# First FFN's context rounded and subtracted one place earlier, attention steps divided anew, bias added later

## The reference

```python
x = x + 0.5 * ffn(layernorm(x))
x = x + attn(layernorm(x))        # 16 heads of 8, qkv and output bias
x = x + 0.5 * ffn(layernorm(x))

def ffn(x):                       # a switch head: H = 8 heads, E = 8 experts, P = 128
    gate_v, gate_o = top2_gates(x @ sel_v_w.T), top2_gates(x @ sel_o_w.T)
    q, k = x @ q_w.T, x @ k_w.T                       # by head
    v = sum_e (x @ v_w[h, e]) * gate_v[..., h, e]
    ctx = softmax(q @ k.T / sqrt(128)) @ v
    return sum_he (ctx[h] * gate_o[..., h, e]) @ o_w[h, e]
```

## Time and profile before

| | |
|---|---|
| three runs | 1562.11, 1564.19, 1565.19 us; median 1564.19 |
| the profiled execution | 1565.24 us; span of its instructions 1563.5 us |
| busy | PE 94%, DVE 84%, ACT 77%, POOL 62% of the span |
| mean granted clock of PE | 0.976 of full speed |
| first FFN's slots, up to the first attention score | to 660 us |
| last slots of the first FFN with 30 attention steps | 660 to 711 us |
| attention alone | 711 to 905 us |

### The profile page before, as it was taken

One profiled execution on the slowest core, in us unless ns is written; L12 is line 12 of the kernel. 1 busy time (PEld: TensorE's weight loads), 2 busy tenths in 40 slices (PEclk: granted clock), 3 DMA queues, 4 the chain that ended last, 5 costly groups with the idle time before them and its releaser, 6 DMA issues. The chain is left out here.

```text
span 1563.5 us, 25918 instructions
## 1 busy us (share of the span) xinstructions
PE 1474.1 (94%) x7227; PEld 1101.0 (70%) x7227; DVE 1308.9 (84%) x3532; ACT 1209.7 (77%) x3587; POOL 976.3 (62%) x1719
## 2 busy tenths in 40 slices
PE   4898999999999999978988899999999999999997
PEld 3577778888888888743333347888888888888884
DVE  6989889988998877868898948988898889887884
ACT  3677888888888888737886687888888888888884
POOL 3477887777777776642332125777677767776665
PEclk8899999999999999979998999999999999999999
DMA  6144433333343235301211012233233233333321
GB/s 196 41 162 148 162 135 109 108 109 108 109 135 109 108 109 202 109 27 68 72 55 64 27 55 82 108 109 108 109 115 109 108 109 115 110 115 116 125 83 34
DMA packets 50838, 163.49 MB, mean 105 GB/s; under 512 B 3460, under 2 KB 26630, under 8 KB 34310
## 3 DMA queue, kind: packets, MB, share of 16 engines
q1 hardware_dynamic: 50694, 161.82, 29.8%
HBM read 136.64 MB, written 25.17 MB: 103 GB/s over the span
## 5 line engine op out<-in xcount | busy, mean ns | idle before, releaser
L989 ACT ACTIVATE vt<-bank,gate 128x128 f32<-128x128 f32 x1024 | 293.3, 372 | 169.1 <-PE bank L520 152.1
L1349 DVE SCALAR_TENSOR_TENSOR ot<-bank,gn,ot 128x128 f32<-128x128 f32 x1024 | 288.1, 344 | 82.7 <-ACT ot L1028 51.3
L1636 POOL TENSOR_TENSOR vt<-vt 128x256 f32<-128x256 f32 x256 | 193.7, 757 | 240.9 <-DVE vt L1335 240.7
L1028 ACT ACTIVATE ot<-bank,gn 128x128 f32<-128x128 f32 x1024 | 292.6, 371 | 41.9 <-PE bank L520 31.7
L1335 DVE SCALAR_TENSOR_TENSOR vt<-bank,gate,vt 128x128 f32<-128x128 f32 x1024 | 286.0, 342 | 12.3 <-ACT vt L989 10.6
L1661 POOL TENSOR_TENSOR ot<-ot 128x256 f32<-128x256 f32 x256 | 200.9, 785 | 100.2 <-DVE ot L1349 95.6
L1358 DVE TENSOR_TENSOR pt<-bank,pt 128x512 fp32r<-128x512 f32 x256 | 175.9, 687 | 74.9 <-ACT pt L1016 74.3
L518 PE MATMUL bank<-wv,xhl 128*128 128x512 f32 x512 | 225.8, 441 | 13.4 <-ACT vt L989 12.0
L518 PE MATMUL bank<-wo,chl 128*128 128x512 f32 x512 | 208.6, 407 | 21.8 <-DVE chl L1318 19.6
L1005 ACT ACTIVATE pp<-bank,nmin 128x512 f32<-128x512 f32 x256 | 180.5, 705 | 36.6 <-DVE nmin L1325 34.4
L1325 DVE TENSOR_REDUCE nmin<-bank 128x1 f32<-128x512 f32 x256 | 173.9, 679 | 39.8 <-PE bank L520 37.8
(11 more groups left out here) (192 smaller groups left out, 3039.8 us busy)
## 6 DMA issues: line engine op xcount, KB each, us to landing
wv<-wv_split SPq DMA_DIRECT2D x56, 1024.0 KB, 4.9
wo<-wo_split SPq DMA_DIRECT2D x56, 1024.0 KB, 4.8
wv_split<-wv SPq DMA_DIRECT2D x8, 1024.0 KB, 5.1
wo_split<-wo SPq DMA_DIRECT2D x8, 1024.0 KB, 7.1
qk<-qk_rows SPq DMA_DIRECT2D x32, 256.0 KB, 2.9
qk_rows<-qs SPq DMA_DIRECT2D x24, 256.0 KB, 3.0
rawv<-in_L_ffn_v_w SPq DMA_DIRECT2D x8, 512.0 KB, 6.8
rawo<-in_L_ffn_o_w SPq DMA_DIRECT2D x8, 512.0 KB, 8.8
```

Of the source, the lines that this page charges most:

```text
L989: last = activation(vt[:, u % 2, e * P:(e + 1) * P], gb[0][:, e * P:(e + 1) * P], ACT.Copy, scale=gate[:, n % 2, k, h * E + e:h * E + e + 1])
L1028: last = activation(ot[:, u % 2, e * D:(e + 1) * D], gb[2][:, e * D:(e + 1) * D], ACT.Copy, scale=gn[:, j % 2, k, e:e + 1])
L1349: last = v.scalar_tensor_tensor(o, gb[3][:, e * D:(e + 1) * D], gn[:, j % 2, k, G + e:G + e + 1], o, ALU.mult, ALU.add)
L1636: own.link(g_.tensor_tensor(a[:, 0:2 * P], a[:, 0:2 * P], a[:, 2 * P:4 * P], ALU.add))
```

## The change

In ACT's and DVE's slots the context of head g - 1 is handled at the end of slot 4g + 3 and no longer at the start of slot 4g + 4. Between these two places stand, on DVE, `split_values` and `prepare` of slot 4g + 3, and on both engines the attention steps that `SCHEDULE` puts after slots 127 and 131. The 30 steps are divided anew over the slots. `add_constant` moves from step 10 to step 44 of its batch.

```diff
-STEPS_BESIDE = {125: 2, 126: 2, 127: 2, 128: 4, 129: 4, 130: 4, 131: 3, 132: 3, 133: 3, 134: 3}
+STEPS_BESIDE = {125: 2, 126: 2, 127: 4, 128: 3, 129: 3, 130: 3, 131: 4, 132: 3, 133: 3, 134: 3}
@@ ACT, slot(t)
-                    if k == 0 and 2 <= g < HEADS + 2:
-                        context(g - 2)
...
                     if 0 <= t - O_BEHIND < TILES:
                         outputs(t - O_BEHIND)
+                    if k == QT - 1 and 1 <= g <= HEADS:
+                        context(g - 1)
@@ POOL, step(s)
-                    if batch_of(s, 10) is not None:
+                    if batch_of(s, 44) is not None:
                         add_constant(b)
```

## The result

The changed kernel takes 1556.3 us (median of 8 runs, 1553.04 to 1558.27) against 1561.45 for the kernel before (8 runs); ratio 0.9957, 95% interval 0.9947 to 0.9967. By this ratio it is 0.43% faster; the two medians alone differ by 5.15 us, 0.33%. A large part of this is the yardstick: the three runs shown had a median of 1564.19, the eight have 1561.45, and the profiled execution of before (1565.24) was slower than all eight. Trace against trace the two spans differ by 1563.5 - 1554.6 = 8.9 us, where my sum was 4.5.

What follows compares the result with a forecast made beforehand. PE was taken as the bound, busy 464.30 of 465.00 us from 190 to 655 us. Terms -1.85 - 2.8 + 2.05 - 1.9 = -4.5 us gave 1560.7 (profile) and 1559.7 (median), middle 1560.2; range 1557.2 to 1564.3.

Steps and rivals of the forecast that it cites:

- Context in front of split and preparation: Heads 1 to 5: context starts earlier on DVE, part of the gain becomes a wait for pt_rest; 1.85 us faster.
- The clock in the body: Two early low-clock stretches of PE, behind waits of 2.49 and 2.39 us, vanish; 2.8 us faster, bounds 0 and 2.8.
- rival 2: The gain is eaten: early low stretches stay or before's median lacks them; -1.7 us, 1563.0, no change; chance 0.20.
- Normalise later: Five slots where normalise now follows the context, so PE's transposes wait longer: 0.60 + 4 x 0.36 = 2.05 us lost.
- The last slots: End of the first FFN, slots 127 to 131, context earlier and steps redivided: outputs(124) 1.9 us earlier, bounds 0 and 4.3.
- the upper bound of 4.3: Most the last slots could gain: 1.9 us plus the lower clock in slot 132, 2.3 to 2.4 us.
- The rival that the second stretch would vanish: Rival of the last slots: the tail's second low-clock stretch goes too, 2.3 us more, 1557.9; chance 0.17.
- the 1.2 us that I charged to PE: Slot 127: PE stands until row maximum 4 is done, so outputs(120) start 1.2 us late.
- The bias: `add_constant` on POOL moved 34 steps back: nobody waits for it, 0 us taken, bounds 0 and 1.3 lost.
- Attention: Stage behind the change: limited by DVE, waits for no fixed time, so the advance passes through.
- Where the clock falls: Gate counting runs freely, so falls vary between runs; up to 2.8 us of gain might not show in a median.

Runs made afterwards that it cites:

- tail_only: Kernel before with the context moved for heads 30 and 31 of the first FFN alone, and the new division of steps; 1558.68 us, ratio 0.9974.
- steps_only: Kernel before with the steps divided anew over the slots, context and bias as before; 1564.39 us, ratio 1.0012.
- bias_only: Kernel before with only `add_constant` moved to step 44; 1562.56 us, ratio 0.9998.
- norm_first: Changed kernel, but in the slots that normalise DVE takes the context behind `prepare`, as before; 1551.98 us, ratio 0.9921.
- body_only: Kernel before with the context moved for heads 0 to 29 of the first FFN and all of the second, old steps and bias; 1556.7 us, ratio 0.9974.
- before_warm: Kernel before with idle matmuls on PE in front of its waits for `chl` (heads 1 to 4, 30, 31); 1560.82 us, ratio 0.9967.

## Why the prediction was right or wrong

**The starting point.** The forecast is 4.5 us below 1564.7, the middle between the profiled execution and the median of three. The eight runs of before have 1561.45, 3.25 lower, and the three later sets of them 1562.67 to 1563.54. That alone carries most of the 3.9 us between 1560.2 and 1556.3: against the median of eight the change gives 5.15 us, 0.65 more than my sum. But the sum was worked out on one profile, and against this profile 8.9 were measured. Its terms, one by one:

**Context in front of split and preparation** was right in kind and partly in size. The waits for `chl` turned into waits for pt_rest, at slot 12 at 1.07 + 1.16 us where I had 1.25 + 1.2. With the clock held up in both orders the advance at head 4 is 167.85 - 166.74 = 1.1 us, where I had 1.85.

**The clock in the body**: 2.8 us forecast, and 170.67 - 167.85 = 2.8 measured against the profile of before. But tail_only, steps_only and bias_only, with the body of before, had one such stretch and not two (their context(5, 0) stands 1.6 to 2.1 us earlier), so against a median some 1.4 to 2.1 is counted too much, and rival 2 was half right. The reason that I gave, waits shorter than any behind which the clock fell, doesn't hold by itself either: PE and clock in steps_only, at slot 12 and in the second FFN:

```profile
101.64 0.50 PE L518 MATMUL bank<-wo,chl 128*128 128x512 f32 x1 [2.49 <-DVE chl L1318]
...
103.14 0.39 PE L698 MATMUL bank<-pt,vv 128*128 128x512 f32 x1
...
1530.76 0.69 PE L518 MATMUL bank<-wo,chl 128*128 128x512 f32 x1 [2.16 <-DVE chl L1318]
1531.25 0.63 PE L519 MATMUL bank<-wo,chl 128*128 128x512 f32 x1
```

Behind the same 2.49 us, at the same instruction, the clock fell in before and not here; behind 2.16 us it fell here, and behind 2.19 at the same instruction of before (1537.62) it didn't. That both stretches went with the change was seen in every profile of it, but why is not shown.

**Normalise later**: 2.05 us forecast, 1.0 + 0.55 measured by norm_first. Behind the context L1171 took 0.96 us instead of 1.03 near 223 us, and near 378 us 0.92 instead of 1.01; the four small losses were 0.3 and not 0.36. I ranked it right: it is the one part of the change that costs, and taking it back is what makes a better kernel.

**The last slots** are the term that failed, mis-sized at 1.9 us: "Following PE slot by slot I get outputs(121) at 680.2 (now 679.95), (122) at 685.5 (now 685.56), (123) at 688.7 (now 690.01): the advance sits in slot 130", and with it the 1.9 us and the upper bound of 4.3. Measured were 5.8 between the marks, trace against trace. I carried the lower clock of before, up to 682.7, into the changed kernel. At it PE's own work sets the pace, and a step less per slot hardly shows. In the changed kernel the stretch behind slot 127 ended at 673.9. Once the clock is up, the fourth step's wait is what a slot hangs on: in the rows without low stretches slots 128, 129 and 130 go from 4.5, 5.1 and 4.5 us to 3.0, 4.2 and 2.8, 4.1 us in all; slots 127 and 131 pay 0.3 and 0.1. So of the 5.8 us about 4.0 are order and division. The other 1.8 are the clock: low stretches of 9.2 and 6.2 us (by the lengths of matmuls), which cost before 75.7 - 70.8 = 4.9, became two of 3.1 and 2.7, which cost the changed kernel 69.9 - 66.8 = 3.1. The rival that the second stretch would vanish was wrong (it came at 687.9, after a wait of 1.73), and what I called its gain came from the first one.

In slot 127 the 1.2 us that I charged to PE were 0.3, since the transposes behind step 7 still ran at 2.4 GHz (0.41 us to the first output matmul and not 1.04).

**The bias**: 0, right.

**Attention** passed the advance on within 0.3 us, right. But it isn't as steady as I took it: over all profiles the stage takes 171.2 to 177.4 us. In before and in both profiles of the changed kernel PE has a second low stretch some 160 us behind the first quotient, and the stage takes 174.3 to 174.5 us; in body_only, tail_only, steps_only, bias_only and norm_first it has none, and takes 171.3 to 171.4. Before_warm has the longest, with a third low stretch near 765 us, so that its profile keeps 3.5 us behind it of the 732.00 - 725.54 = 6.5 won up to the first quotient. What decides it isn't settled; before and changed kernel have it alike, so it explains none of their difference.

**Where the clock falls.** The Trainium skill (TensorE: Matmul & The Clock Gate, "Part 1: The HAM clock gate") says that the gate's counting runs on freely and isn't restarted by the kernel; it says of the rise at a kernel's start that its place varies by this, and the prediction carried it over to the fall. The two profiles of the changed kernel differ by 0.3 us at most: their low stretches begin at 670.8 and 687.9 and at 670.7 and 687.8 us. But before, tail_only, steps_only and bias_only run the same instructions up to slot 124, and they do differ (low near 103 and 127 us, against near 124 alone), as such a rule would have it. Whether the rule is the cause isn't shown.

## What to carry to other kernels

When an order is changed on the engine that PE waits for, look at every item that is pushed back, not only at what is pulled forward: one reader of one pushed item cost some 1.5 us where the body had gained 4.0, and was had back by one condition. And don't carry a low-clock stretch of the old trace into the forecast of the new one: work the chain out at both clocks, for at the lower one PE's own work hides what the order is worth. Nor take one profile for the kernel: this one was slower than each of the eight runs.

## What the hardware showed

PE's clock can fall behind a short wait: in before_warm, at 676.34 us, 1.6 us after a wait of 1.23 us between attention scores of 32 rows. And the length of a wait didn't decide it: at one and the same instruction of the second FFN, among full products, the clock fell behind 2.16 us in steps_only and in bias_only and stayed at 2.4 GHz behind 2.19 us in before, and at slot 12 it fell behind 2.49 us in before and stayed behind 2.49 us in those two. Matmuls whose results are thrown away, 49 and then 12 more of them, made the kernel before 0.33% and 0.44% faster by their ratios (0.17% and 0.40% by the medians); in the profiles the low stretches that they stood in front of are gone.
